# A mixture-of-experts kernel: experts in falling order of count, weights loaded and split inside the tile stage, gathers in four buffers, and a first part that keeps x and h on the chip

## The chip, the cores and the metric

The kernel runs on one core of a Trainium2 chip. A core has TensorE (PE: matrix products; the loading of a stationary operand has rows of its own, PEld), VectorE (DVE), ScalarE (ACT), GpSimd (POOL), and SyncE (SP), which here only issues transfers. 16 DMA engines move the data. Each engine runs its own program in order; they wait for one another on semaphores. The metric is the device time in microseconds.

## What is computed

x has 8 batches of 512 tokens of 256 numbers. Cut from the reference, with B = 8, D = 256, E = 8 experts, FF = 1024 and two experts for each token:

```
h = (x - mu) * rsqrt(var + 1e-05) * ln_g + ln_b            # over the 256 numbers of a token
h_norm = (h - h.mean(1)) * rsqrt(h.var(1) + 1e-08)         # over the 512 tokens of a batch
se = subj_emb[subject_ids]
hyp = relu(se @ hyp_w1 + hyp_b1) @ hyp_w2 + hyp_b2
sty = relu(hyp @ sty_w1 + sty_b1) @ sty_w2 + sty_b2
gamma, beta = split(sty, 2);  gamma = softplus(gamma) + 1e-08
h = h_norm * gamma + beta
probs = softmax(h @ router_w);  gates, idx = top_k(probs, 2);  gates = gates / gates.sum(-1)
hid  = relu(h @ exp_w1[e] + exp_b1[e])
eout = hid @ exp_w2[e] + exp_b2[e]
out  = x + sum over the two experts e of gate * eout
```

## The kernel before, in words

The 8192 pairs of a token and an expert are sorted by expert, each expert's list is filled up to whole tiles of 128, and TILES = 71 tiles are worked through. The program has two stages.

*First part.* For each of the 8 batches of x: statistics of each token (token_stats, VectorE), normalising (normalise, ScalarE), transposing on TensorE (transposes), gain and offset on the way out of PSUM (affine, ScalarE), statistics over the tokens (time_stats, VectorE), modulation with gamma and beta (modulate, GpSimd), logits and transposing back (logits, back, TensorE), copying the rows (rows, ScalarE) and storing them with SyncE into h_rows in memory. x and h have two buffers each on the chip; GpSimd loads x and writes it to out_rows, to which the tiles are added later. Beside this SyncE loads all weights (16 units of 1 MB, one for each of w1 and w2 of an expert) into four stages; ScalarE writes the fp16 high half of a unit (w_hi, 2048 columns) and VectorE the low half (w_lo). Then select picks the two experts of each token, the counts come from a product with ones, and VectorE works out where each expert's list begins. The gates (comb) are stored beside the rows in h_rows.

*Tile stage.* Tile t needs its 128 token numbers (slot_steps and the tokens functions on VectorE, slot_table on TensorE), a gather of the rows by an indirect transfer of GpSimd (gather), two transposes (tile_transpose), halves in fp16 (tile_hi on ScalarE, tile_lo on VectorE), the hidden products (48 of 128 columns) and relu, halves again (split_hi, split_lo), the second products (24 of 256 columns), bias_y on VectorE, the gate (gate_y, ScalarE), and an indirect transfer of GpSimd that adds the 128 rows to out_rows (scatter). Each product of fp32 numbers is three products of fp16 halves.

The order on each engine is written out by hand. In step t TensorE does products(0) (hidden of tile t, first half; second products of tile t-2), tile_transpose(t+1), slot_table(t+3) and products(1). ScalarE does relu of the first half, tile_hi(t+1), gate_y(t-2) and relu of the second half. GpSimd's loop is, before:

```
for t in range(4, TILES + 2):
    scatter(t - 2, (t - 2) % 2)
    if t + 3 < TILES:
        gather(t + 3, (t + 3) % 2)
```

The gathered rows have two buffers, and gather(t+3) waits until the gates of tile t+1 are read (s_gate). scatter(t) waits for yout of its tile (s_yo, by gate_y) and for the landing of the scatter before (s_sc). Ahead of each indirect transfer stands a tiny tensor_tensor that writes held_gp and carries its waits (carry). The line numbers of the profile: 390 gather, 401 scatter, 298 carry, 397 the copy of the scatter's index, 657 tile_transpose, 647 slot_table, 691 and 698 the products, 524 relu, 531 tile_hi, 538 gate_y, 852 w_lo, 474 w_hi, 567 transposes, 577 back, 586 logits, 468 rows, 455 affine.

Of the kernel before, what the change touches and what calls it, by code (L numbers as in the profile page):

```python
# [12 lines left out]
P = 128  # L24
# [18 lines left out]
NSTAGE = 4  # L43
VEC_ROWS = 75
V_LNG, V_LNB, V_HB1, V_HB2, V_SB1, V_SB2 = 64, 66, 68, 69, 70, 71


C_ID, C_SLOT, C_NEGT, C_SLOTCOL, C_Q, C_DJ, C_DESC, C_TOK2, C_T128 = 0, 128, 256, 328, 400, 401, 405, 413, 415
C_END = C_T128 + 72


def moe_kernel(nc, x, ids, ln_g, ln_b, subj_emb, hyp_w1, hyp_b1, hyp_w2, hyp_b2, sty_w1, sty_b1,
               sty_w2, sty_b2, router_w, exp_w1, exp_b1, exp_w2, exp_b2, consts, consts16, out):
# [9 lines left out]
    def w_v(u):  # L63
        return (w2_v if u % 2 else w1_v)[u // 2]

    with ExitStack() as ctx:
# [7 lines left out]

        whi = sb("whi", [P, UNITS * UNIT], F16)
        wlo = sb("wlo", [P, UNITS * UNIT], F16)
        stage = sb("stage", [P, NSTAGE, UNIT])
        cst = sb("cst", [P, C_END])
        c16 = sb("c16", [P, 2 * P], F16)


        xs = sb("xs", [P, 2, JB * D])
        xn = sb("xn", [P, 2, JB * D])
        hT = sb("hT", [P, 2, KD * T])
        hrow = sb("hrow", [P, 2, JB * D])
        hid32 = hT
        hidhi = stage[:, 1, 0:FF].bitcast(F16).rearrange("p (a f) -> p a f", a=2)
        hidlo = stage[:, 2, 0:FF].bitcast(F16).rearrange("p (a f) -> p a f", a=2)
        b2row = hrow[:, :, :].rearrange("p a n -> p (a n)")
        hg = xs[:, 0, 0:2 * HROW].rearrange("p (a d) -> p a d", a=2)  # L90
        ysum = xn[:, 0, 2 * D:4 * D].rearrange("p (a d) -> p a d", a=2)
        yout = xs[:, 1, 0:2 * D].rearrange("p (a d) -> p a d", a=2)
        hThi = xn[:, 0, 0:D].bitcast(F16).rearrange("p (a d) -> p a d", a=2)
        hTlo = xn[:, 0, D:2 * D].bitcast(F16).rearrange("p (a d) -> p a d", a=2)
        step16 = xn[:, 1, 0:2 * P].bitcast(F16).rearrange("p (a h s) -> p a h s", a=2, h=NH)
        junk = xn[:, 1, 2 * P:3 * P]


        hw1 = hrow[0:SE, 1, 0:SH]
        hw2 = hrow[:, 1, SH:2 * SH]  # L100
        sw1 = hrow[:, 1, 2 * SH:2 * SH + SH // 2]
        sw2 = hrow[0:SH // 2, 1, 320:320 + 2 * D]

        d1, d2, ex, oh1 = (xs[:, 0, i * NBLK:(i + 1) * NBLK] for i in range(4))
        tm = xn[:, 1, 3 * P:5 * P]
        sums = xn[:, 1, 5 * P:7 * P]
        csum, dstart = xn[:, 0, 2 * D:3 * D], xn[:, 0, 3 * D:4 * D]
        ones = xn[:, 0, 0:NBLK]
        ge = xs[:, 1, 0:72 * E]


        vrows = sb("vrows", [P, P])
        vcol = sb("vcol", [P, VEC_ROWS])
        rw = sb("rw", [P, KD * E])
        idcol = sb("idcol", [B, 1], I32)
        se = sb("se", [B, SE])
        sT = sb("sT", [P, 4, B])
        gam = sb("gam", [P, KD * B])
        bet = sb("bet", [P, KD * B])
        sp = sb("sp", [P, 6, KD * B])  # L120
        bns = sb("bns", [P, JB, 6])
        mv = sb("mv", [P, 2, JB, 2])
        lnv = sb("lnv", [P, 2, 4, JB])
        tns = sb("tns", [P, KD, 6])
        tmv = sb("tmv", [P, 2, KD, 2])
        tnv = sb("tnv", [P, 2, 6, KD])
        lg = sb("lg", [P, NJ * E])
        selh = sb("selh", [P, NBLK + 1], F16)
        dsel = sb("dsel", [P, NBLK], F16)
        m8 = sb("m8", [P, 8, NJ])  # L130
        start = sb("start", [P, NBLK + 1])
        ne = sb("ne", [P, 6, E])
        nei = sb("nei", [P, 2, E], I32)
        stcol = sb("stcol", [P, 2 * NH])
# [998 lines left out]
```

## Time and profile before

| | |
|---|---|
| median of 3 runs | 545.5 us (543.27 to 732.71) |
| the profiled execution | 544.19 us |
| its span in the trace | 542.5 us |
| TensorE busy | 465.7 us (86%), 5671 instructions |
| VectorE busy | 399.0 us (74%) |
| ScalarE busy | 290.7 us (54%) |
| GpSimd busy | 280.5 us (52%) |
| moved by the DMA engines | 51.36 MB, mean 95 GB/s |

The profile shows one execution. The span goes from its first to its last instruction; the execution's time holds some 1.7 us more. Shares of busy time are means over both stages, so they don't say what bounds either of them; the rows below are taken from single stretches. A busy share of an engine counts neither the issue of plain transfers nor waiting.

### The profile page before, as it was taken

How to read it: one execution, taken by the hardware profiler on the slowest of the kernel's cores; microseconds unless marked ns; L12 is line 12 of the kernel's file. 1: busy time of each engine (PE TensorE's matmuls, PEld its weight loads, DVE VectorE, ACT ScalarE, POOL GpSimd, SP SyncE). 2: the span in 40 equal slices, each digit the busy share in tenths (PEclk: the TensorE clock that was granted, in tenths of full speed). 3: DMA queues.
4: the chain of work that ended last, by engine and by line, in shares of the span. 5: the costliest groups of instructions: out<-in, count | busy, mean ns of one | idle time of the engine just before them, and what ended most of it. 6: DMA issues, size and time to landing. Idle time of an engine off the chain costs nothing.

```text
span 542.5 us, 16211 instructions
## 1 busy us (share of the span) xinstructions
PE 465.7 (86%) x5671; PEld 437.9 (81%) x5671; DVE 399.0 (74%) x1488; ACT 290.7 (54%) x819; POOL 280.5 (52%) x426
## 2 busy tenths in 40 slices
PE   1357666707999999999999999999999999999990
PEld 1356656606999999999999999999999999999990
DVE  3688998897677787777777777777777777877650
ACT  2879877703555455554555545555555554555540
POOL 5032223545465566565665556565556556665542
PEclk9999999999999999999999999999999999999997
DMA  8989996241232322323223232232322323223221
GB/s 270 342 310 323 343 357 213 45 130 29 36 50 50 52 48 48 49 52 51 47 47 51 52 51 47 47 51 51 51 46 48 51 49 53 45 49 51 50 32 19
DMA packets 36417, 51.36 MB, mean 95 GB/s; under 512 B 7804, under 2 KB 29718, under 8 KB 36214
## 3 DMA queue, kind: packets, MB, share of 16 engines
q0 software_dynamic: 16128, 27.59, 25.9%
q1 hardware_dynamic: 20214, 22.78, 12.9%
q8 instruction: 47, 0.77, 0.6%
q14 instruction: 28, 0.23, 0.1%
HBM read 32.24 MB, written 18.11 MB: 93 GB/s over the span
## 4 chain that ended last, share of the span: by engine, by line
PE 76%; DVE 9%; issue 5%; DMA 4%; ACT 2%; POOL 2%; DVEq 0%; POOLq 0%; ACTq 0%
PE bank L691 34%; PE bank L698 33%; PE bank L657 3%; DMA out_rows<-xs 2%; PE bank L647 1%; PE bank L586 1%; DMA xs<-h_rows,idxg 1%; PE bank L567 1%; ACT whi L474 1%; DVE wlo L852 1%; POOL out_rows L401 1%; DMA xs<-in_x 1%; POOL hT L319 1%; DVE xn L950 1%; PE bank L577 1%
## 5 line engine op out<-in xcount | busy, mean ns | idle before, releaser
L698 PE MATMUL bank<-whi,stage 128*128 x1136 | 276.9, 273 | 0.0
L524 ACT ACTIVATE hT<-bank,vcol 128x128 f32<-128x128 f32 x568 | 162.4, 368 | 194.1 <-PE bank L691 194.0
L691 PE MATMUL bank<-xn,whi 128*128 128x128 f16 x2272 | 220.3, 220 | 2.2 <-DVE xn L1004 1.1
L691 PEld LDWEIGHTS bank<-xn,whi 128*128 x2272 | 171.6, 98 | 15.7 <-issue 4.8
L691 PE MATMUL bank<-xn,wlo 128*128 128x128 f16 x1136 | 156.7, 220 | 0.0
L698 PE MATMUL bank<-wlo,stage 128*128 x568 | 154.8, 273 | 0.0
L401 POOL DMA_INDIRECT out_rows<-xs,idxs x71 | 119.4, 1681 | 24.3 <-issue 24.3
L1010 DVE CAST stage<-hT 128x512 f16<-128x512 f32 x142 | 62.0, 437 | 75.6 <-ACT hT L524 61.0
L698 PEld LDWEIGHTS bank<-whi,stage 128*128 128x128 f16 x1136 | 111.1, 98 | 6.6
L298 POOL TENSOR_TENSOR held_gp<-zero 1x1 f32<-1x1 f32 x150 | 36.2, 241 | 133.5 <-DVE tok L996 100.7
L1015 DVE TENSOR_TENSOR stage<-hT,stage 128x512 f16<-128x512 f32 x142 | 96.9, 682 | 0.1
L390 POOL DMA_INDIRECT xs<-h_rows,idxg x71 | 71.0, 1000 | 35.0 <-issue 33.3
L691 PEld LDWEIGHTS bank<-xn,wlo 128*128 x1136 | 87.7, 98 | 0.0
L698 PEld LDWEIGHTS bank<-wlo,stage 128*128 128x128 f16 x568 | 55.6, 98 | 0.1
L1020 DVE SCALAR_TENSOR_TENSOR xn<-bank,hrow 128x256 f32<-128x256 f32 x71 | 30.2, 425 | 20.9 <-PE bank L698 20.9
L968 DVE TENSOR_SCALAR xn<-cst,stcol 128x128 f16<-128x128 f32 x142 | 42.3, 340 | 0.0
L577 PE MATMUL bank<-cst,hT 128*128 128x128 f32 x64 | 15.7, 426 | 29.5 <-POOL hT L319 28.2
L538 ACT ACTIVATE xs<-xn,gates 128x256 f32<-128x256 f32 x71 | 37.8, 532 | 3.1 <-DVE xn L1020 3.1
L577 PEld LDWEIGHTS bank<-cst,hT 128*128 128x128 f32 x64 | 12.7, 226 | 32.3 <-POOL hT L319 22.0
L531 ACT ACTIVATE xn<-bank 128x256 f16<-128x256 f32 x71 | 28.4, 400 | 14.8 <-PE bank L657 14.8
L852 DVE SCALAR_TENSOR_TENSOR wlo<-stage,whi 128x2048 f32 (+1 forms) x14 | 32.0, 2290 | 1.1 <-ACT whi L474 0.4
L657 PE MATMUL bank<-cst,xs 128*128 128x128 f32 x142 | 27.7, 277 | 3.8 <-DMA xs<-h_rows,idxg 3.8
(145 smaller groups left out, 500.3 us busy)
## 6 DMA issues: line engine op xcount, KB each, us to landing
stage<-in_L_cond_exp_w SPq DMA_DIRECT2D x16, 1024.0 KB, 8.6
xs<-in_x POOLq DMA_DIRECT2D x8, 512.0 KB, 6.6
out_rows<-xs POOLq DMA_DIRECT2D x8, 512.0 KB, 7.8
h_rows<-hrow SPq DMA_DIRECT2D x8, 512.0 KB, 10.6
xs<-h_rows,idxg POOLq DMA_INDIRECT x71
out_rows<-xs,idxs POOLq DMA_INDIRECT x71
hrow<-in_L_cond_exp_b SPq DMA_DIRECT2D x1, 1024.0 KB, 4.7
cst<-in_consts SPq DMA_DIRECT2D x1, 243.5 KB
```

Of the source, the lines that this page charges most:

```text
L298: gp.tensor_tensor(held_gp[:, kind:kind + 1], zero[0:1, 0:1], zero[0:1, 0:1], ALU.add).then_inc(s_held[kind], 1)
L390: gp.indirect_dma_start(out=hg[:, par, :], out_offset=None, in_=h_dram, in_offset=bass.IndirectOffsetOnAxis(ap=idxg[par][:, 0:1], axis=0)) ...
L401: gp.indirect_dma_start(out=out, out_offset=bass.IndirectOffsetOnAxis(ap=idxs[par][:, 0:1], axis=0), in_=yout[:, par, :], in_offset=None, ...
L524: ins = nc.scalar.activation(hid32[:, par, c * P:(c + 1) * P], bk_hid[half][:, (c - 4 * half) * P:(c - 4 * half + 1) * P], ACT.Relu, bias= ...
L538: nc.scalar.activation(yout[:, par, :], ysum[:, par, :], ACT.Copy, scale=gates[:, bass.ds(t, 1)]).then_inc(s_yo, 1)
L657: ins = nc.tensor.transpose(bk_g[:, k * P:(k + 1) * P], hg[:, par, k * P:(k + 1) * P], ident)
L691: hid_ins = nc.tensor.matmul(o, lhs[w, k], h[:, par, k * P:(k + 1) * P], start=(n == 0), stop=(n == 3 * KD - 1))
L698: y_ins = nc.tensor.matmul(bk_y[par_y][:, 0:D], h[:, par_y, c * P:(c + 1) * P], rhs[w], start=(n == 0), stop=(n == 3 * FC - 1))
L852: V.scalar_tensor_tensor(out=wlo[:, bass.ds(at, UNIT)], in0=stage[:, slot, :], scalar=WSCALE, in1=whi[:, bass.ds(at, UNIT)], op0=ALU.mult, ...
L968: ins = V.tensor_scalar(step16[:, par, h, :], slotrow, stcol[:, h:h + 1], cst[:, bass.ds(t + C_NEGT, 1)], ALU.subtract, ALU.is_ge)
L1010: V.tensor_copy(hidhi[:, par, a:b], hid32[:, par, a:b]).then_inc(s_dv, 1)
L1015: V.tensor_tensor(hidlo[:, par, a:b], hid32[:, par, a:b], hidhi[:, par, a:b], ALU.subtract).then_inc(s_split, 1)
```

## The change

What it does, part by part:

- *Order of the experts.* After the counts, VectorE sorts the experts by falling count (a key of count and number, max), publishes their numbers in nei (s_ord), and copies the eight parts of selh into that order (selp). SyncE, ScalarE and VectorE read numbers from it into registers. Tiles then come in the order of ranks, and weights lie by rank in whi and wlo.
- *Weights.* None is loaded in the first part. After s_ord SyncE loads eight quarters of the first two units, then stores comb, and loads the other 14 units of 1 MB behind waits for w_lo (three stages). ScalarE and VectorE split the first eight quarters ahead of the tile stage, and in each step t of the tile stage quarter t + 8 (512 columns): w_hi between gate_y and the second relu, w_lo at the end of VectorE's step. GpSimd no longer splits any.
- *First part.* x (8 batches) and h stay on the chip, in the place where weights will lie. Parameters come in one transfer, laid out on the host. Statistics and modulation go by pairs of batches. GpSimd normalises x in place; the statistics over the tokens are read from PSUM; gain, offset and modulation become one pass on ScalarE (modulate). out_rows is filled from x by transfers from memory to memory. Subjects are picked by a product with a one-hot matrix. Probabilities are not divided by their full sum before the two are chosen, since that factor cancels.
- *Gathers.* The gathered rows get four buffers, hg; gather(t) waits for the gates of tile t-4. Four gathers are issued before the loop, and in the loop scatter(t-2) is followed by gather(t+2). The scatter takes its index from tok without a copy.

The diff, cut to the loops of the tile stage, the loading and the splitting:

```diff
+            sp_.wait_ge(s_ord, 1)
+            order = expert_numbers(sp_, nei[0:1, 2, :])
...
+            for i, (u, q) in enumerate(FIRST):
+                src = w_src(u, q)
+                sp_.dma_start(stage[:, u, q * CHUNK:(q + 1) * CHUNK].rearrange("p (a n) -> p a n", a=src.shape[1]),
+                              src).then_inc(s_first[i], 16)
             for part, batches in enumerate((range(0, B - 2), range(B - 2, B))):
...
                 sp_.wait_ge(s_comb, part + 1)
                 for b in batches:
...
+                    sp_.dma_start(comb_v[b], comb[:, b * JB * E:(b + 1) * JB * E].rearrange("p (j e) -> p j e", e=E)).then_inc(s_combst, 16)
+            for u in range(2, UNITS):
+                if u >= NSTAGE:
+                    sp_.wait_ge(s_wlo, NQ * (u - NSTAGE + 1))
+                src = w_src(u)
+                sp_.dma_start(stage[:, u % NSTAGE, :].rearrange("p (a n) -> p a n", a=src.shape[1]), src).then_inc(s_w[u % NSTAGE], 16)
...
+            def normalise(b):
+                gp.wait_ge(s_nrm, b // 2 + 1)
...
-            def gather(t, par):
...
+            def gather(t):
                 gp.wait_ge(s_tok, t + 1)
-                if not (isinstance(t, int) and t < 2):
-
-                    gp.wait_ge(s_gate, t - 1)
+                if t >= 4:
+                    gp.wait_ge(s_gate, t - 3)
                 carry(t, 0)
-                gp.indirect_dma_start(out=hg[:, par, :], out_offset=None, in_=h_dram,
-                                      in_offset=bass.IndirectOffsetOnAxis(ap=idxg[par][:, 0:1], axis=0)).then_inc(s_gh[par], 16)
...
+                gp.indirect_dma_start(out=hg[:, t % 4, :], out_offset=None, in_=h_dram,
+                                      in_offset=bass.IndirectOffsetOnAxis(ap=tok[:, t:t + 1], axis=0)).then_inc(s_gh[t % 4], 16)
...
-                gp.tensor_copy(idxs[par][:, :], tok[:, bass.ds(t, 1)]).then_inc(s_idx, 1)
-                gp.wait_ge(s_idx, t + 1)
                 gp.wait_ge(s_yo, t + 1)
                 carry(t, 1)
...
-            for t in range(5):
-                if t == 2:
-
-                    last_w_lo(1)
-                gather(t, t % 2)
-            for t in range(2, 4):
-                scatter(t - 2, t % 2)
-                gather(t + 3, 1 - t % 2)
-            for t in range(4, TILES + 2):
-                scatter(t - 2, (t - 2) % 2)
-                if t + 3 < TILES:
-                    gather(t + 3, (t + 3) % 2)
+            for t in range(4):
+                gather(t)
+            gp.wait_ge(s_init, 16 * B)
+            for t in range(2, TILES + 2):
+                scatter(t - 2)
+                if t + 2 < TILES:
+                    gather(t + 2)
             gp.wait_ge(s_sc, 16 * TILES)
...
+            for b in range(0, B, 2):
+                time_deviation(b // 2)
+                modulate(b)
+                modulate(b + 1)
...
+                rows(b)
+                rows(b + 1)
...
+                relu(t, t % 2, 0, es[2 + t % 4])
+                if t + 1 < TILES:
+                    tile_hi(t + 1, 1 - t % 2)
+                if t >= 2:
+                    gate_y(t - 2, t % 2)
+                if t + len(FIRST) < UNITS * NQ:
+                    w_hi(t + len(FIRST))
+                relu(t, t % 2, 1, es[2 + t % 4])
...
+                V.scalar_tensor_tensor(out=wlo[:, at], in0=stage[:, u % NSTAGE, q * CHUNK:(q + 1) * CHUNK], scalar=WSCALE, in1=whi[:, at],
+                                       op0=ALU.mult, op1=ALU.subtract).then_inc(s_wlo, 1)
...
+                if t + len(FIRST) < UNITS * NQ:
+                    w_lo(t + len(FIRST))
```

GpSimd's program, before, where the gathers that are issued ahead end and the loop begins. held_gp is the carrier of the waits, DMA xs<-h_rows a gather, DMA out_rows<-xs a scatter. The rows are gather(4), scatter(0), gather(5) and scatter(1):

```order
L298 TENSOR_TENSOR held_gp<-zero 1x1 [waits gather_waits_carried,gates_ready,slot_tokens_ready]
L390 DMA xs<-h_rows,idxg0 128x264
L397 COPY idxs0<-tok 128x1
L298 TENSOR_TENSOR held_gp<-zero 1x1 [waits y_gated,scatter_index_ready]
L401 DMA out_rows<-xs,idxs0 4232x256
L298 TENSOR_TENSOR held_gp<-zero 1x1 [waits gather_waits_carried,gates_ready,slot_tokens_ready]
L390 DMA xs<-h_rows,idxg1 128x264
L397 COPY idxs1<-tok 128x1 [waits y_scattered]
L298 TENSOR_TENSOR held_gp<-zero 1x1 [waits scatter_waits_carried,y_gated,scatter_index_ready]
L401 DMA out_rows<-xs,idxs1 4232x256
```

The same place in the changed kernel, with DMA hg<-h_rows a gather: gather(3), scatter(0), gather(4), scatter(1) and gather(5):

```order
L300 TENSOR_TENSOR held_gp<-zero 1x1 [waits gather_waits_carried,slot_tokens_ready]
L307 DMA hg<-h_rows,tok 128x264
L300 TENSOR_TENSOR held_gp<-zero 1x1 [waits y_gated,out_initialised]
L316 DMA out_rows<-yout,tok 4232x256
L300 TENSOR_TENSOR held_gp<-zero 1x1 [waits gather_waits_carried,gates_ready,slot_tokens_ready]
L307 DMA hg<-h_rows,tok 128x264
L300 TENSOR_TENSOR held_gp<-zero 1x1 [waits scatter_waits_carried,y_gated,y_scattered]
L316 DMA out_rows<-yout,tok 4232x256
L300 TENSOR_TENSOR held_gp<-zero 1x1 [waits gather_waits_carried,gates_ready,slot_tokens_ready]
L307 DMA hg<-h_rows,tok 128x264
```

The copies to idxs are gone, and what follows scatter(0) is gather(4) instead of gather(5).

ScalarE's program in one step of the tile stage, before. The first row is tile_hi, the second gate_y, the others relu of the second half; an ISA row is a piece of register work:

```order
L531 ACTIVATE xn<-bank4 128x256 [waits tile_transposed]
L538 ACTIVATE xs<-xn,gates 128x256 [waits y_scattered,y_biased]
L524 ISA [waits hidden_products]
L524 ACTIVATE hT<-bank1,vcol 128x128
L524 ISA
L524 ACTIVATE hT<-bank1,vcol 128x128
L524 ISA
L524 ACTIVATE hT<-bank1,vcol 128x128
L524 ISA
L524 ACTIVATE hT<-bank1,vcol 128x128
```

ScalarE's program in a step of the changed kernel, again from tile_hi on, then into the first relu of the next step:

```order
L424 ACTIVATE hThi<-bank4 128x256 [waits tile_transposed]
L430 ACTIVATE yout<-ysum,gates 128x256 [waits y_scattered,y_biased]
L412 ACTIVATE whi<-stage 128x512 [waits weights_staged0]
L418 ACTIVATE hid32<-bank1,par 128x128 [waits hidden_products]
L418 ACTIVATE hid32<-bank1,par 128x128 x3
L418 ACTIVATE hid32<-bank0,par 128x128 [waits hidden_products]
```

Behind gate_y stands the high half of a quarter of a weight unit; the order of tile_hi and gate_y is what it was.

## Rows read from the trace of the kernel before

**Rows 1.** Busy time of each engine by stretches: two of 31 and 197 us.

```profile
core 0: us, PE busy (x) PEld busy (x) DVE busy (x) ACT busy (x) POOL busy (x), PEclk, DMA share, GB/s
29.00:60.00 31.00, 20.94 (x96) 19.75 (x96) 28.08 (x78) 25.38 (x38) 7.69 (x14) 1.00 0.94 327
...
133.00:330.00 197.00, 196.96 (x2652) 186.47 (x2650) 146.18 (x590) 102.44 (x348) 116.28 (x172) 1.00 0.29 48
```

**Rows 2.** Timeline of PE: the transposes of steps 2, 31 and 69 (start, us).

```profile
138.37 0.38 PE L657 MATMUL bank<-cst,xs 128*128 128x128 f32 x2
...
302.29 0.38 PE L657 MATMUL bank<-cst,xs 128*128 128x128 f32 x2
...
517.15 0.38 PE L657 MATMUL bank<-cst,xs 128*128 128x128 f32 x2
```

**Rows 3.** Timeline of ACT, step 31: tile_hi and gate_y.

```profile
303.27 0.40 ACT L531 ACTIVATE xn<-bank 128x256 f16<-128x256 f32 x1
303.53 0.53 ACT L538 ACTIVATE xs<-xn,gates 128x256 f32<-128x256 f32 x1
```

**Rows 4.** Timeline of POOL: a slow carrier, and gather and scatter of one step.

```profile
157.44 0.72 POOL L298 TENSOR_TENSOR held_gp<-zero 1x1 f32<-1x1 f32 x1
158.32 1.61 POOL L401 DMA_INDIRECT out_rows<-xs,idxs  x1 [0.16 <-issue]
...
302.34 0.18 POOL L298 TENSOR_TENSOR held_gp<-zero 1x1 f32<-1x1 f32 x1 [1.35 <-DVE tok L996]
303.02 0.99 POOL L390 DMA_INDIRECT xs<-h_rows,idxg  x1 [0.49 <-issue]
304.00 0.20 POOL L397 COPY idxs<-tok 128x1 int32<-128x1 int32 x1
304.29 0.18 POOL L298 TENSOR_TENSOR held_gp<-zero 1x1 f32<-1x1 f32 x1
304.89 1.73 POOL L401 DMA_INDIRECT out_rows<-xs,idxs  x1 [0.42 <-issue]
```

**Rows 5.** The chain that ended last, 119 to 133 us: two gathers, issue to landing.

```profile
119.26 3.06 DMA xs<-h_rows,idxg
...
122.37 0.70 PE bank L657 x2
...
129.90 2.73 DMA xs<-h_rows,idxg
```

**Rows 6.** All scatters of line 401: ns min/median/max, first and last start.

```profile
L401 POOL DMA_INDIRECT out_rows<-xs,idxs x71: 1567/1718/1975, 141.0 to 534.3; - x71
```

**Rows 7.** Groups of instructions: w_lo of a unit, and split_lo (busy us, mean ns).

```profile
L1015 DVE TENSOR_TENSOR stage<-hT,stage 128x512 f16<-128x512 f32 x142 | 96.9, 682 | 0.1
...
L852 DVE SCALAR_TENSOR_TENSOR wlo<-stage,whi 128x2048 f32 x12 | 27.5, 2291 | 0.9 <-ACT whi L474 0.2
```

**Rows 8.** Timeline of the first part: back, logits, rows, affine of one batch.

```profile
30.65 1.97 PE L577 MATMUL bank<-cst,hT 128*128 128x128 f32 x8 [10.48 <-POOL hT L319]
...
32.41 3.42 PE L586 MATMUL bank<-rw,hT 128*128 128x8 f32 x16
...
35.09 1.05 ACT L468 ACTIVATE hrow<-bank 128x512 f32<-128x512 f32 x2
...
37.67 1.45 ACT L455 ACTIVATE hT<-bank,vcol 128x512 f32<-128x512 f32 x2 [1.44 <-PE bank L567]
```

**Rows 9.** Timeline between the stages: stores of comb, a VectorE subtraction, the first products.

```profile
104.10 4.25 SPq L272 DMA_DIRECT2D h_rows<-xs  x6
...
109.72 4.16 DVE L950 TENSOR_TENSOR xn<-start 128x256 f32<-128x256 f32 x1
...
124.42 0.60 PE L691 MATMUL bank<-xn,whi 128*128 128x128 f16 x4 [1.15 <-DVE xn L1004]
```

**Rows 10.** Timeline of PE: four hidden products early in the tile stage.

```profile
125.03 0.63 PE L691 MATMUL bank<-xn,whi 128*128 128x128 f16 x4
...
128.73 0.39 PE L691 MATMUL bank<-xn,whi 128*128 128x128 f16 x4
...
130.84 0.39 PE L691 MATMUL bank<-xn,whi 128*128 128x128 f16 x4 [0.94 <-issue]
```

More of the change, by code:

```diff
@@ L337, in _ @@
+            for b in range(B):
+                normalise(b)
             held = [0]
@@ L625, in _ @@
-            for b in range(B - 2, B):
-                back(b, b % 2)
-            pe.wait_ge(s_cst16, 16)
-            pe.wait_ge(s_sel, 2)
-            nc.tensor.matmul(bk_cnt[:, 0:NBLK], ones16, selh[:, 1:NBLK + 1], start=True, stop=True).then_inc(s_cnt, 1)
+            pe.wait_ge(s_cst16, 16)
+            pe.wait_ge(s_par, 16)
+            pe.wait_ge(s_hot, 1)
+            MM(bk_small[0:SE, 0:B], subj, onehot[:, 1, :], start=True, stop=True).then_inc(s_sty_pe, 1)
+            pe.wait_ge(s_sty_a, 1)
@@ new lines, in _ @@
+            ins.then_inc(s_sty_pe, 1)
+            pe.wait_ge(s_cst, 16)
+            transposes(0)
+            transposes(1)
+            for b in range(0, B - 2, 2):
+                transposes(b + 2)
+                transposes(b + 3)
+                for i in (b, b + 1):
+                    logits(i)
+                    back(i)
+            for b in (B - 2, B - 1):
+                logits(b)
+            for b in (B - 2, B - 1):
+                back(b)
+            pe.wait_ge(s_sel, 2)
@@ new lines, in _ @@
+            link(ins)
+            for k in range(E):
+                ins = V.tensor_copy(selp[:, 1 + k * NJ:1 + (k + 1) * NJ], selh[:, bass.ds(order[k] * NJ, NJ)])
+            ins.then_inc(s_perm, 1)
+            ve.wait_ge(s_perm, 1)
+            V.tensor_tensor(dsel[:, :], selp[:, 1:NBLK + 1], selp[:, 0:NBLK], ALU.subtract).then_inc(s_ds, 1)
+            ve.wait_ge(s_ccol, 1)
+            V.tensor_tensor(ca16[:, :], bk_col[:, 0:NH], adj[:, 0, :], ALU.add).then_inc(s_ca, 1)
+            ve.wait_ge(s_col, 1)
@@ L1044, in _ @@
                 if t == 0:
-                    tile_experts()
-                if t == 1:
-                    tile_lo(0, 0)
-            ve.wait_ge(s_b2, 16)
-            def step(t, par, at, e, e_y):
-                def tile(u):
-                    return not isinstance(u, int) or 0 <= u < TILES
-                other, tokens = 1 - par, tile(t + 3)
-                gate(t, par, e)
-                if tile(t - 2):
-                    bias_y(t - 2, par, e_y)
-                if tile(t + 4):
+                    w_lo(0)
+                    w_lo(1)
+            w_lo(2)
+            w_lo(3)
+            tile_lo(0, 0)
+            for i in range(4, 8):
+                w_lo(i)
+            tile_experts()
+            at += 1
+            tile_experts_done(at)
+            ve.wait_ge(s_b2, 16)
+            es = [order[0]] * 6
+            for t in range(TILES):
+                if t >= 8 and t % 4 == 0:
+                    if t == 8:
+                        ve.wait_ge(s_et, 1)
+                    es = expert_numbers(ve, etile[0:1, t:t + 6])
+                par, other, tokens = t % 2, 1 - t % 2, t + 3 < TILES
+                gate(t, es[2 + t % 4])
+                if t >= 2:
+                    bias_y(t - 2, par, es[t % 4])
+                if t + 4 < TILES:
                     slot_steps(t + 4, par)
```

1087 lines of the change are left out of this document (498 added, 589 removed).

## The prediction

> **What bounds the kernel now.** I read the stretches first, to see which stage is bound by what. While h is built (29 to 60 us) TensorE is busy 20.94 of 31 us and the DMA engines 0.94 of the time; in the tile stage TensorE is busy 196.96 of 197 us, VectorE 146.18, ScalarE 102.44 and GpSimd 116.28 [rows 1]. So up to about 100 us the transfers set the pace, and from 133 us on TensorE does. Its pace in that stage is read from the pair of transposes that stands in the middle of each step. Call the time at which step t transposes tile t+1 M(t). M(2) is 138.37 and M(69) is 517.15, so 67 steps take 378.8 us, 5.65 each [rows 2]. The kernel before is therefore M(2) = 138.4, plus 67 times 5.65, plus 25.35 from M(69) to the end of the span: 542.5. Then I read GpSimd's row of events in one step, because it starts both indirect transfers of a tile and the change rewrites its loop.
>
> **The one step that decides: the gather has moved by one tile.** In both kernels ScalarE's step t does, in order, relu, tile_hi(t+1), which needs M(t), and gate_y(t-2); GpSimd's scatter(t-2) waits for that gate_y. In step t the trace shows M(t) at 302.29 [rows 2], tile_hi(t+1) at 303.27, gate_y(t-2) at 303.53 [rows 3], and scatter(t-2) starting at 304.89, which is M(t) + 2.6 [rows 4]. Before, what follows it on GpSimd is gather(t+3), whose rows are first needed at M(t+2), 11.3 us after M(t). Now it is gather(t+2), needed at M(t+1). Four row buffers instead of two don't help, since the queue on GpSimd is a fixed order. So a closed chain appears that goes round once per tile: M(t), tile_hi(t+1), gate_y(t-2), scatter(t-2), gather(t+2), M(t+1). Its length, from rows:
> - rows landed to TensorE's start, 0.05: a gather that starts at 119.26 lands 3.06 later, and the transposes start at 122.37 [rows 5];
> - the two transposes, 0.38 [rows 2];
> - tile_hi to the start of gate_y, 0.26, and gate_y, 0.53 [rows 3];
> - held_gp before the scatter to the scatter's start, 0.60 (304.29 to 304.89), and 0.88 where held_gp itself ran long (157.44 to 158.32) [rows 4];
> - the scatter's own time on GpSimd, 1.72 by its median [rows 6];
> - held_gp before the gather to the gather's start, 0.68 (302.34 to 303.02) [rows 4];
> - the gather's start to its landing, 3.06 and 2.73 [rows 5]; I take 2.9.
>
> That is 0.05 + 0.38 + 0.79 + 0.60 + 1.72 + 0.68 + 2.9 = 7.12; three more handovers between engines at the 0.05 of the first line give 7.25 us, against 5.65. The copy to idxs (0.20 [rows 4]) is already left out. The shortest chain (2.73, no handovers) is 6.95, the longest (0.88, 3.06, handovers) 7.7, and a gather that shares the DMA engines with a weight transfer may be later still: 7.9. Every one of them is above 5.65, so TensorE stops in front of the transposes of each tile for about 1.6 us. The first four gathers are issued ahead, and gather(4) is the first one behind a scatter, which is needed at M(3); so the chain holds from M(2) to M(69): 67 x 7.25 = 486 us instead of 379, **+107 us**.
>
> The Trainium skill, "DMA: Bandwidth & Descriptors", Anatomy of one DMA — SWDGE (gpsimd) path, gives 2.0 us plus bytes / 436e3 for such a transfer, some 2.3 us for 128 rows of 1,056 bytes. By it the chain would be 6.65 and the result about 608 us; this case's gathers took 2.73 and 3.06, so the measurement decides.
>
> **The other parts of the change.**
> - Splitting weights in the tile stage. Each of the first 56 steps gets one w_hi of 512 columns on ScalarE and one w_lo on VectorE. A whole w_lo took 2.29 us for 2048 columns, a tensor_tensor of 512 columns 0.68 [rows 7]: I take 0.68. VectorE's load per tile is 146.18 / 197 x 5.65 = 4.19 [rows 1]; less the index that is written twice today (0.15, an estimate), plus 0.68, it is 4.7, under 5.65 and far under 7.25: nothing. Without that cover it would cost at most 56 x 0.68 = 38 us. ScalarE has still more room. The split lies behind the last index of a step, so the instruction that queues behind it is the next tile's gate and bias_y.
> - Loading weights there: 14 transfers of 1 MB where the queues are slack. They wait on w_lo and nothing but weights waits behind them on SyncE. Chunk 8r + 3 is split in step 8(r - 1) + 3 and needed in step 8r: five steps early.
> - The products: the same 48 and 24 matmuls per tile, no gain. Registers of expert numbers are read at the same steps.
> - The new first part. It drops 16 MB of weights, so the transfers no longer bound it; a serial chain per pair of batches does. ScalarE takes rows(2i+1) before the square root of the next pair: 1.05, about 1.3 for the root and the five small VectorE steps behind it (an estimate), modulate 1.45, two batches of transposes at 1.97, and logits and back for two batches, 2 x (3.42 + 1.97) [rows 8]: 18.5 us a pair. With the first logits at about 38 us (statistics of two pairs and the style network lie ahead; 35 to 42), the third pair's back ends at 86, the last rows are transposed back at about 101, near 105.4 before. From there the first index took until 118; the instruction of 4.16 us is gone [rows 9], while the sorting of the experts, the register reads and the eight copies of selh come in, some 4 us. SyncE now issues eight weight pieces and only then the eight stores of comb, at 4.25 / 6 = 0.7 each [rows 9], before the first gather may start: it starts at 114 to 118. From a first gather (119.26 [rows 5]) to the first product (124.42 [rows 9]) it is 5.2, and 13.95 more to M(2). So M(2) lies at 133 to 137; I take 135, a gain of 3, and 127 to 145 as its bounds.
> - The end: three scatters, each behind the landing of the one before; two index copies less, 0.4.
>
> **Sum.** 135 + 486 + 25.35 - 0.4 = 646 us of span; the profiled execution took 544.19 for its 542.5, so + 1.7 = **648 us**. The median of the runs, 545.5, stands 1.3 above that execution. A measurement of this kernel can tell about 2% from no change, 11 us.
>
> **Rivals.**
> - The gather comes in time after all. It decides at 1.6 us: if a gather landed 1.3 us after its start, or if a scatter held GpSimd for 0.1 us, the chain would be 5.65 and TensorE would be the bound again: 135 + 379 + 25 + 1.7 = 541, and some 545 if every fourth step, where experts are read, delays tile_lo. Against it stand both landings and a scatter row that never falls under 1.57 [rows 6]. This is also the case in which the change is not slower. 8%.
> - TensorE's clock falls because of the new stops. Four products take 0.63 us at 125.03 and 0.39 at 128.73; after a stop of 0.94 they still take 0.39 [rows 10]. Where TensorE was idle a third of the time, a batch's eight transposes took 1.97, 0.22 apart [rows 8], while two take 0.38 in the tile stage [rows 2]. So 1.2 GHz comes back somewhere between a stop of 0.94 us in steady work and the first part's pattern, and 1.6 us per 7.25 lies between. The granted clock of both stretches reads 1.00 [rows 1], so it is the durations that show it. At 1.2 GHz a tile is 11.3; with half of the steps there, 135 + 67 x 9.3 + 27 = 785 us. The Trainium skill, "TensorE: Matmul & The Clock Gate", A second HAM failure mode: psum-queue depth-cycling, reports this for frequent short stops; the gap at 130.84 speaks against it. 7%.
> - The first part gains much more, say 25 us, because its pairs overlap better. Even then it is 623; it can't turn the sign.
>
> **Chances.** The chain as the bound has 85%. Its range takes 6.95 with M(2) at 127 and 7.9 with 145: 127 + 466 + 27 = 620 and 145 + 529 + 27 = 701. Both named rivals lie outside, 15%, and I leave 4% for sizes past the ends. Faster by over 2% has 3%, within 2% has 5%, slower 92%.
>
> **What would show it.** Right: a wait of TensorE's transposes for the gathered rows on 66 or more tiles, 1.3 to 2.2 us each; TensorE's share of the tile stage near 78%; step spacing of 7.25; scatter and gather next to each other on GpSimd, which then waits for gate_y. Wrong: spacing of 5.65 with transposes that never wait, or four products at 0.6 us in the middle of the tile stage.

## The result, and the profile after

The changed kernel takes 647.2 us (median of 4 runs, 644.1 to 653.2) against 544.4 us: ratio 1.191, 95% interval 1.179 to 1.203. The forecast was 648. The profiled execution took 644.08 us, its span is 642.2. Below, medians are over all executions of a kernel while ratios leave out those more than 1.5% above its fastest; their first part came later, so the tile stage is compared by its own spacing.

First the stretches, as in [rows 1], from the windows view of the changed kernel:

```profile
29.00:60.00 31.00, 19.01 (x128) 18.54 (x128) 21.41 (x93) 10.61 (x19) 9.55 (x19) 0.84 0.36 122
133.00:330.00 197.00, 163.23 (x2075) 147.15 (x2073) 127.70 (x462) 97.13 (x301) 88.88 (x109) 0.98 0.35 76
```

The DMA share of the first stretch has fallen from 0.94 to 0.36: the weights are gone from there. In the tile stage no engine is full any more. TensorE, busy 196.96 of 197 us before, is busy 163.23, or 83%. When every engine has room and the stage is longer, something goes round. The waits say where it closes (who waited for whom, us in total, times, longest):

```profile
POOL held_gp L300 <- issue: 242.9, 68, 4.6
...
PEld bank L543 <- DMA hg<-h_rows,tok: 110.9, 62, 10.8
PE bank L543 <- DMA hg<-h_rows,tok: 93.6, 62, 10.5
```

Line 543 is the pair of transposes of a tile. It waits for gathered rows on 62 tiles, 10.5 of the 93.6 us once, for tile 0. GpSimd in turn waits 68 times in front of a scatter, 3.6 us on average. The view names no releaser for it ("issue"), but held_gp, which carries the wait for gate_y, starts 0.13 or 0.14 us after the end of gate_y in each of 67 steps. The transposes themselves, from the timeline of TensorE; they answer to [rows 2]:

```profile
130.91 0.38 PE L543 MATMUL bank<-cst,hg 128*128 128x128 f32 x2
138.47 0.44 PE L543 MATMUL bank<-cst,hg 128*128 128x128 f32 x2 [1.76 <-DMA hg<-h_rows,tok]
...
303.90 0.44 PE L543 MATMUL bank<-cst,hg 128*128 128x128 f32 x2 [1.06 <-DMA hg<-h_rows,tok]
310.81 0.44 PE L543 MATMUL bank<-cst,hg 128*128 128x128 f32 x2 [1.05 <-DMA hg<-h_rows,tok]
...
617.26 0.44 PE L543 MATMUL bank<-cst,hg 128*128 128x128 f32 x2 [1.07 <-DMA hg<-h_rows,tok]
```

M(2) is 130.91 and M(69) 617.26, so a step takes 486.35 / 67 = 7.26 us, and 25.0 us lie behind M(69). The stop begins at M(3), the first tile whose gather is queued behind a scatter.

One round of the chain, between the two rows in the middle: first two of ScalarE's rows, then GpSimd's.

```profile
304.38 0.38 ACT L424 ACTIVATE hThi<-bank 128x256 f16<-128x256 f32 x1 [0.59 <-PE bank L543]
304.66 0.50 ACT L430 ACTIVATE yout<-ysum,gates 128x256 f32<-128x256 f32 x1
```

```profile
305.29 0.61 POOL L300 TENSOR_TENSOR held_gp<-zero 1x1 f32<-1x1 f32 x1 [3.24 <-issue]
306.06 1.60 POOL L316 DMA_INDIRECT out_rows<-yout,tok  x1 [0.16 <-issue]
307.11 0.61 POOL L300 TENSOR_TENSOR held_gp<-zero 1x1 f32<-1x1 f32 x1
307.96 1.00 POOL L307 DMA_INDIRECT hg<-h_rows,tok  x1 [0.24 <-issue]
```

Read downwards: transposes at 303.90, tile_hi 304.38, gate_y 304.66, held_gp 305.29, scatter 306.06, gather 307.96, and the next transposes, which need the rows of that gather, at 310.81. The pieces are 0.48, 0.28, 0.63, 0.77, 1.90 and 2.85: 6.91 us. Between scatter and gather GpSimd rests for 0.24.

7.26 is a mean over unequal steps. Of 67, 37 take 6.80 to 7.05 and 30 take 7.27 to 8.26: there a gather landed late, or TensorE was slow behind a longer stop, or the scatter came later after M(t). The section on the prediction returns to these.

### The profile page after: what moved, and what is told of

Its sections match the earlier page's. It is cut to its first block and busy times, and to the rows that moved or that the text cites. A ratio compares the mean times of both kernels' runs of the same rounds, so it can differ in the third digit from the quotient of the medians.

```text
span 642.2 us, 15826 instructions
## 1 busy us (share of the span) xinstructions
PE 477.2 (74%) x5679; PEld 431.7 (67%) x5679; DVE 386.0 (60%) x1436; ACT 282.6 (44%) x832; POOL 251.2 (39%) x331
## 5 line engine op out<-in xcount | busy, mean ns | idle before, releaser
L418 ACT ACTIVATE hid<-bank,par 128x128 f32<-128x128 f32 x568 | 161.9, 368 | 213.0 <-PE bank L588 213.0
L588 PE MATMUL bank<-hThi,whi 128*128 128x128 f16 x1136 | 191.4, 222 | 5.3 <-DVE hTlo L843 4.4
L588 PE MATMUL bank<-hTlo,whi 128*128 128x128 f16 x1136 | 191.6, 222 | 0.0
L588 PE MATMUL bank<-hThi,wlo 128*128 128x128 f16 x1136 | 159.1, 222 | 0.0
L595 PE MATMUL bank<-whi,hidhi 128*128 (+1 forms) x568 | 157.3, 277 | 0.0
L595 PE MATMUL bank<-wlo,hidhi 128*128 (+1 forms) x568 | 157.3, 277 | 0.0
L595 PE MATMUL bank<-whi,hidlo 128*128 (+1 forms) x568 | 156.9, 276 | 0.0
L588 PEld LDWEIGHTS bank<-hThi,whi 128*128 (+1 forms) x1136 | 112.4, 99 | 14.7 <-DVE hTlo L843 5.0
L316 POOL DMA_INDIRECT out_rows<-yout,tok x71 | 114.2, 1608 | 14.0 <-issue 13.6
L588 PEld LDWEIGHTS bank<-hTlo,whi 128*128 (+1 forms) x1136 | 112.9, 99 | 6.2
L543 PE MATMUL bank<-cst,hg 128*128 128x128 f32 x142 | 31.0, 300 | 93.6 <-DMA hg<-h_rows,tok 93.6
```

The lines of the kernel that those rows point to most:

```text
L316: gp.indirect_dma_start(out=out, out_offset=bass.IndirectOffsetOnAxis(ap=tok[:, t:t + 1], axis=0), in_=yout[:, t % 2, :], in_offset=None, ...
L418: ins = S(hid32[:, par, c * P:(c + 1) * P], bk_hid[half][:, (c - 4 * half) * P:(c - 4 * half + 1) * P], ACT.Relu, bias=vcol[:, bass.ds(e * ...
L543: ins = nc.tensor.transpose(bk_g[:, k * P:(k + 1) * P], hg[:, t % 4, k * P:(k + 1) * P], ident)
L588: hid_ins = MM(o, lhs[w, k], h[:, par, k * P:(k + 1) * P], start=(n == 0), stop=(n == 3 * KD - 1))
L595: y_ins = MM(bk_y[par_y][:, 0:D], h[:, par_y, c * P:(c + 1) * P], rhs[w], start=(n == 0), stop=(n == 3 * FC - 1))
```

## Experiments

**1. The gather in front of the scatter.** If the chain is closed by the order of two calls, turning them round opens it: the gather then waits for neither scatter nor gate_y.

```diff
             for t in range(2, TILES + 2):
-                scatter(t - 2)
                 if t + 2 < TILES:
                     gather(t + 2)
+                scatter(t - 2)
```

> The changed kernel with one thing moved: in GpSimd's loop gather(t+2) stands ahead of scatter(t-2) instead of behind it. Theory A, the closed chain over scatter and gather: it is cut, the transposes never wait for rows, the step spacing is 5.65 us, and with the changed kernel's M(2) = 130.9 and its end, 24.8, the span is 131 + 67 x 5.65 + 25 = 535 us, the time 537. Theory B, the stops come from the weight transfers and the splitting that now lie in the tile stage: spacing stays above 6.9 us and the time above 620 us.

Measured: 554.5 us (546.0 to 558.0, 8 runs), ratio 1.013 (1.008 to 1.017); M(2) is 143.11 and M(69) 531.56, so 5.80 us a step. Two swapped calls give back 98 of 108 us (67 times 7.26 less 5.80, and less 5.65). The rest was not expected, and 554.5 misses theory A's 537: transposes still waited ten times, up to 1.17 us, and M(2) came 12 us late.

**2. The old distance.** Five gathers ahead of the loop, and gather(t+3) behind the scatter, as the kernel before does, in the changed kernel.

```diff
-            for t in range(4):
+            for t in range(5):
                 gather(t)
...
-                if t + 2 < TILES:
-                    gather(t + 2)
+                if t + 3 < TILES:
+                    gather(t + 3)
```

> The changed kernel with the old lead: five gathers ahead and gather(t+3) behind scatter(t-2), with the four buffers and all the rest as changed. Theory A: gather(t+3) now waits for the token numbers of the step, but is needed 11.3 us after M(t); 5.65 us a step and 537 us, as in the run beside it, within 3 us. Theory B: above 620 us.

552.7 us (546.2 to 556.3, 4 runs), 5.79 us a step from M(2) = 136.01. The chain is gone here too, and the same 0.14 us a step over the kernel before is left, so this run misses its 537 as well. The two experiments are less different than they look. In both the gather starts as soon as its token numbers are there, in most steps 5.0 to 5.4 us before the transposes that need it; gather(t+3) doesn't start a step earlier than gather(t+2) does in experiment 1.

**3. The chain alone, in the kernel before.** Nothing of the change but the distance: four gathers ahead and gather(t+2) behind the scatter, with the old first part and no weights in the tile stage.

```diff
-            for t in range(5):
+            for t in range(4):
...
-                if t + 3 < TILES:
-                    gather(t + 3, (t + 3) % 2)
+                if t + 2 < TILES:
+                    gather(t + 2, (t + 2) % 2)
```

> The kernel before with the new lead alone: four gathers ahead and gather(t+2) behind scatter(t-2); weights, first part, two buffers and the index copy stay as before. Theory A: the chain appears here too, 6.9 to 7.3 us a step, so 138 + 67 x (6.9 to 7.3) + 25 + 2 = 627 to 654 us. Theory B: no weights move in this tile stage, so 544 us stay.

653.3 us, ratio 1.201 (1.199 to 1.204): the whole loss, and a little more, from this edit. M(2) is 137.68, M(69) 626.40: 7.29 us a step, a mixture of 34 steps of 6.87 to 7.04 and 33 of 7.1 to 8.1, as in the changed kernel. The loss appears in full without the splitting, the loading and the new first part.

**4. A longer chain.** A fill of 768 columns with its wait, between scatter and gather.

```diff
                 scatter(t - 2)
                 if t + 2 < TILES:
+                    link(gp.memset(par_[:, P_HW1:P_HW1 + 768], 0.0))
                     gather(t + 2)
```

> The changed kernel with a memset of 768 columns and its wait on GpSimd between scatter(t-2) and gather(t+2), some 0.9 to 1.1 us by the 0.34 us that a memset of 264 columns took in the first part. Theory A: it lies in the chain, so every step from M(2) to M(69) grows by its length: 60 to 75 us more than the changed kernel, 705 to 722 us. If GpSimd had room there: under 5 us more.

719.8 us, 8.29 a step: +1.03 for a fill that takes 1.32 and partly runs beside the scatter. From M(t) to the gather's start it is 5.04 us on average in place of 4.12, so 0.92 of the 1.03 lie where the fill was put; the other 0.12 are gathers that took longer to be used.

**5 and 6. Weights in quarters.** In experiment 1 the late gathers stood beside weight transfers. Its rows, from the timelines of GpSimd, SyncE's queue and TensorE:

```profile
271.30 1.00 POOL L307 DMA_INDIRECT hg<-h_rows,tok  x1 [0.16 <-issue]
...
271.29 0.38 SPq L254 DMA_DIRECT2D stage<-in_exp_w  x1
...
277.94 0.44 PE L543 MATMUL bank<-cst,hg 128*128 128x128 f32 x2 [1.17 <-DMA hg<-h_rows,tok]
```

The gather lands 6.6 us after its start where 2.85 is usual. All ten stops belong to gathers beside which a 1 MB transfer started, 0.01 to 0.18 us earlier. So both orders were run with the same megabytes cut into pieces of 256 KB, one a step:

```diff
-            for u in range(2, UNITS):
+            for i in range(len(FIRST), UNITS * NQ):
+                u, q = i // NQ, i % NQ
...
-                sp_.dma_start(stage[:, u % NSTAGE, :]...).then_inc(s_w[u % NSTAGE], 16)
+                sp_.dma_start(stage[:, u % NSTAGE, q * CHUNK:(q + 1) * CHUNK]...).then_inc(s_w[i % (NSTAGE * NQ)], 16)
```

> The changed kernel with the gather of tile t+2 ahead of the scatter of tile t-2 (as in the earlier run with that order), and the weights of the tile stage loaded in quarters of 256 KB, one a step, in place of 1 MB every fourth step. Theory A: what was left of the step over the kernel before (5.80 against 5.65 us) is gathers that land late because a 1 MB transfer sits in the same DMA engines. With quarters the waits of the transposes shrink to under 0.2 us each, spacing 5.65 to 5.70 us, so the tile stage is 7 to 10 us shorter than with whole megabytes, and the time is 540 to 548 us. Theory B: the waits come of the gather's own long landings, whatever is loaded beside it: spacing stays 5.78 to 5.82 us and the time 550 to 556 us.

542.1 us (10 runs), ratio 0.994 (0.990 to 0.999); no transposes of the loop wait for a gather, 5.67 us a step.

> The changed kernel with five gathers ahead of the loop and gather(t+3) behind scatter(t-2), weights in quarters. Theory A as for the run before: waits of the transposes for the gather vanish (a gather starts a whole step earlier than it is needed), spacing 5.65 to 5.70 us, time 538 to 548 us, which would be level with the kernel before. Theory B: spacing stays at 5.79 us, time 550 to 556 us.

538.0 us (534.6 to 540.9, 4 runs), ratio 0.989 (0.981 to 0.998); M(2) = 129.77, M(69) = 509.68, 5.67 a step. Its windows row, and GpSimd's rows for one step:

```profile
133.00:330.00 197.00, 196.30 (x2641) 185.81 (x2639) 162.93 (x590) 120.37 (x384) 128.04 (x139) 1.00 0.45 94
```

```profile
300.51 0.99 POOL L309 DMA_INDIRECT hg<-h_rows,tok  x1
302.07 0.18 POOL L302 TENSOR_TENSOR held_gp<-zero 1x1 f32<-1x1 f32 x1 [0.57 <-issue]
302.77 1.78 POOL L318 DMA_INDIRECT out_rows<-yout,tok  x1 [0.51 <-issue]
305.71 0.56 POOL L302 TENSOR_TENSOR held_gp<-zero 1x1 f32<-1x1 f32 x1 [1.16 <-DVE tok L831]
306.43 1.16 POOL L309 DMA_INDIRECT hg<-h_rows,tok  x1 [0.15 <-issue]
```

TensorE is full again (196.30 of 197) although it now shares the stage with 14 MB of weights and their split. GpSimd waits for tok ahead of a gather, with time to spare, in place of gate_y. Theory A holds for both. The gathers start 4.9 to 5.6 us before their transposes here too, not a whole step more than in experiment 5 as the expectation has it.

**7 and 8. No weight transfers at all.** In the order of experiment 1 and in the changed kernel, the transfers from the fourth unit on are left out; the stages are split again with what they hold, so most products use wrong weights.

```diff
-            for u in range(2, UNITS):
+            for u in range(2, 3):
...
-                    act.wait_ge(s_w[u % NSTAGE], 16 * len(range(2 + (u - 2) % NSTAGE, u + 1, NSTAGE)))
+                    act.wait_ge(s_w[2], 16)
```

> The kernel with the gather ahead of the scatter, and the plain weight transfers from the fourth unit on left out; the stages are split again with what they hold, so the products use wrong weights and the output is not the reference's. Theory A (the 1 MB transfers delay the gathers): no transpose waits over 0.2 us for a gather, spacing 5.65 to 5.68 us, and the time is 8 to 10 us below the same order with the transfers. Theory B (own long landings): spacing 5.75 to 5.82 us, and the time falls by under 3 us.

545.7 us; 5.67 us a step (M(2) = 138.90, M(69) = 518.97) and no wait for a gather: the same as with quarters. The whole megabytes cost 0.13 us a step, 8 us; cut into quarters they cost nothing.

> The changed kernel itself with the same transfers left out (weights wrong, output not the reference's). Theory A (the chain through scatter and gather sets the step, the transfers have no part in it): spacing 7.15 to 7.3 us, time 636 to 648 us. Theory B (a gather slowed by a weight transfer sets the step): spacing falls to 6.2 us or less, time under 580 us.

644.1 us against 647.2; 7.14 us a step, a hair under the range given. Without the transfers it is 0.12 us a step less, 8 us of a loss of 108, and that is the most that can be put down to them: these are two single executions, and they differ also in how often TensorE was slow behind a stop (6 steps against 3). In the changed kernel the megabyte started some 2 us or more behind the gather that it stood beside, in experiment 1 less than 0.2 us ahead of it. Long landings stay without the transfers.

**9. The fill off the chain.** Experiment 4's fill, in the order of experiment 1.

```diff
                 if t + 2 < TILES:
                     gather(t + 2)
+                    link(gp.memset(par_[:, P_HW1:P_HW1 + 768], 0.0))
                 scatter(t - 2)
```

> The order with the gather of tile t+2 ahead of the scatter of tile t-2, and the same fill of 768 columns with its wait put between the two. In the changed kernel that fill lengthened the step by 1.03 us. Theory A (the step was set by a closed loop through scatter and gather, and with the gather in front that loop is open): the fill only delays the scatter, which nobody waits for; spacing 5.78 to 5.85 us, time 546 to 558 us, that of the same order without the fill. Theory B (GpSimd's own work per step sets the spacing): GpSimd holds about 1 us more in every step, spacing 6.2 us or more, time over 580 us.

571.6 us (571.0 and 572.3), 6.02 us a step: neither theory. The step grew by 0.22 us, not by 1.03 and not by nothing. GpSimd has room, it waits for tok 65 times. The groups of VectorE show where the time is, here and, in the second fence, in experiment 1 (busy us, mean ns):

```profile
L801 DVE TENSOR_SCALAR step<-cst,stcol 128x128 f16<-128x128 f32 x124 | 86.6, 1152 | 0.0
...
L849 DVE CAST hidhi<-hid 128x512 f16<-128x512 f32 x125 | 63.0, 504 | 20.2 <-ACT hid L419 19.1
```

```profile
L848 DVE CAST hidhi<-hid 128x512 f16<-128x512 f32 x129 | 57.1, 442 | 73.2 <-ACT hid L418 73.2
L800 DVE TENSOR_SCALAR step<-cst,stcol 128x128 f16<-128x128 f32 x128 | 39.7, 352 | 0.0
```

The same instruction took 1152 ns in place of 352. Within this run the fill is what tells them apart: 122 of the comparisons from 133 to 530 us overlap a fill and take 1215 ns on average, the 10 that don't take 340. The two of a step overlap each other, so the pair holds VectorE for 86.6 / 62 = 1.40 us in place of 39.7 / 64 = 0.62, some 0.8 more a step, and VectorE, busy 156.39 us between 133 and 330 us in experiment 1, was busy 178.13 here. So this fill wasn't time on GpSimd alone, and experiments 11 and 12 replace it. Nor was it the same time: the fill took 0.75 us here and 1.32 in the chain. In experiment 4 no comparison lay beside a fill, and they took 335 ns.

**10. The version of experiment 6 again,** for a tighter ratio.

> The kernel with gather(t+3) behind the scatter and the weights in quarters once more, for a tighter ratio to the kernel before: 0.985 to 0.995, 535 to 541 us. Its spread comes from the first part, whose pace on TensorE differs from run to run: the tile stage is to take 5.67 us a step in every run, and the time is about 24 us behind M(69).

541.0 us (535.1 to 547.2, 10 runs), ratio 0.991 (0.988 to 0.995). M(2) = 135.13, M(69) = 515.02: 5.67 a step.

**11 and 12. Time on GpSimd without traffic.** Six fills of one column, each with its wait, in the two places.

```diff
+                    for i in range(6):
+                        link(gp.memset(par_[:, P_HW1 + i:P_HW1 + i + 1], 0.0))
```

> The changed kernel with six fills of one column, each with its wait, between the scatter of tile t-2 and the gather of tile t+2: time on GpSimd without the traffic of the 768-column fill. The six should take 0.6 to 1.2 us together. Theory A (closed loop through GpSimd): the step grows by about what they take, less the rest between scatter and gather that they cover, 7.7 to 8.4 us a step, 675 to 725 us. Theory B (the 768-column fill counted in the chain only because it slowed VectorE): the step stays within 0.15 us of 7.26, under 660 us.

760.3 and 783.6 us, above the range; the profile is that of the longer run. M(2) is 138.98 and M(69) 756.48, 9.22 us a step. Theory B has fallen, as the 335 ns of experiment 4 already said, and theory A's size was off. The six took 1.4 to 1.7 us together in place of 0.6 to 1.2. The trace splits the 1.96 us by which the step grew: from M(t) to the gather's start it is 5.68 us in place of 4.12, which is 1.55 for the fills in the chain, and from there to the transposes 3.54 in place of 3.13, which is 0.40 for later landings. Most of the latter is nine steps of 11.5 to 12.5 us, with a stop of some 6. In them a 1 MB transfer starts with the gather, for example at 307.04 and 306.54, and the transposes follow at 312.84. Behind the last of these, from 548 us on, the steps are 8.25 to 9.7.

> The same six fills between gather(t+2) and scatter(t-2) in the order with the gather in front. With the 768-column fill in this place the step was 6.02 us in place of 5.80 and VectorE's counts of slots took 1152 ns in place of 352. Theory A (that fill held VectorE up; time on GpSimd alone is free here): VectorE's counts are back at 350 to 450 ns, spacing 5.75 to 5.85 us, time 546 to 560 us. Theory B (a later scatter costs by itself): spacing stays at 6.0 us or more, 565 us or more.

565.1 and 566.1 us, inside theory B's range for the time but not for the spacing. VectorE's counts are back at 342 ns, as theory A has it, but the mean step is 5.90, above what A gave. Theory A's time was also missed because the first part was late: M(2) is 143.81, as in the 558.0 us execution of experiment 1. There are eleven waits of the loop's transposes for gathers, 0.3 to 1.65 us and 10.9 us together, against ten stops and 5.7 us in experiment 1. All of them stand beside a 1 MB transfer, which starts less than 0.2 us ahead of the gather as it does there; why they are longer was not found. From 425 us on, when the weights are all there, no transposes wait and a step takes 5.71 us against 5.66 in experiment 1. So the six fills, 0.9 us here, cost 0.05 us a step by themselves off the chain, and 1.55 for the 1.4 to 1.7 us that they take in it.

## Why the prediction was right

- **The closed chain, M(t) to gather(t+2) to M(t+1).** Right, and shown from three sides: it appears alone in the kernel before (experiment 3), opens when either call is moved (1 and 2), and pays for what is put in it (4 and 11).
- **Its length, 7.25.** The terms as listed add up to 7.12 + 0.15 = 7.27. The mean is 7.26, but for a reason that is partly luck. A plain round takes 6.91. The term that was too long is scatter to gather: 1.72 + 0.68 = 2.40 in the sum, 1.90 measured. The prediction added the scatter's whole duration from [rows 6] to the held_gp behind it; in the rows above, held_gp starts at 307.11, 1.05 after the scatter's start and inside its 1.60, and nothing stands between the two on GpSimd now. The way from M(t) to the scatter was 2.16 against 0.38 + 0.79 + 0.60 = 1.77 and 0.1 of handovers: the fixed waits between engines were too small. The prediction had a sign of this in its own rows, a scatter at M(t) + 2.6, and didn't ask why its terms gave less. The gather's 2.85 to the transposes was near 2.9 and 0.05. The missing 0.35 x 67 = 23 us came back from things that had been given as ends of the range or as a rival, or not at all: 13.9 us from 14 late gathers, 2.5 from six rounds in which TensorE itself was late, 4.5 from gathers that started later after M(t), the rest in small parts.
- **The later starts.** They are a second length of the chain, which the prediction didn't see. Where TensorE stopped in front of M(t), the scatter starts 2.16 us after it in nearly every step; in the seven steps without such a stop it starts at 2.6, as it did in the kernel before. One of them is M(t) = 210.26: ScalarE's relu of the first half runs from 210.23 to 211.37, so gate_y starts at 211.51 and the scatter at 212.87. The stop had given ScalarE the time to finish that relu first. So a stop shortens the round behind it, by 0.45 us.
- **Late gathers.** The step of 7.9 "that shares the DMA engines with a weight transfer" exists in length, but the weights are a third of the excess at most (7.26 to 7.14 in experiment 8). In the changed kernel the transposes came over 3.5 us after the start of their gather in 14 of 67 steps. (Taken from the gather's start to the transposes' start, which is the landing wherever TensorE was waiting.) In each of the 14 one packet of 16 KB of the queue "q8 instruction" started 1.1 to 2.0 us after the gather, and the transposes came 1.26 to 1.41 us after the end of that packet. In the other 53 no such packet started over 0.2 us after the gather, and they took 2.79 to 3.37; in seven of them one had started earlier or with it. One of the 14, a gather that started at 199.07 (the stretch 199.97 to 202.67 of the DMA view):

```profile
q0 software_dynamic: 152, 0.23, 40.9%
q1 hardware_dynamic: 79, 0.08, 23.0%
q8 instruction: 1, 0.02, 2.1%
...
hg<-h_rows,tok POOLq DMA_INDIRECT x1, 3.8
```

  Without weight transfers (experiment 8) it is again 14 with such a packet, 3.44 to 4.16, the transposes again 1.26 to 1.41 us behind its end, and 53 without, 2.76 to 3.28. So a gather in flight when such a packet moves is used some 0.6 to 1.3 us later than the usual 2.87. That is a coincidence without an exception in 134 gathers; no run took the packets away, so the cause is not shown beyond it.
- **TensorE's clock, a rival at 7%.** It was real in small. After the stop of 2.05 us in front of 202.92, products came 0.42 us long in place of 0.27 until about 206.9, and the step had no wait at the gather behind it because TensorE itself was late:

```profile
202.92 0.44 PE L543 MATMUL bank<-cst,hg 128*128 128x128 f32 x2 [2.05 <-DMA hg<-h_rows,tok]
...
203.75 0.42 PE L595 MATMUL bank<-whi,hidhi 128*128 x1
...
207.28 0.27 PE L595 MATMUL bank<-whi,hidhi 128*128 x1
```

  That happened in 6 of 67 steps, after stops of 1.82 to 2.34 us. It is no clean line: after 8 other stops of 1.84 to 2.19 us the products stayed at 0.27. After shorter ones, 1.06 among them, they always did. It never held for half of the steps, so 785 us was far off.
- **M(2), taken as 135.** 130.91 in the profiled execution; see the section on the first part.
- **Splitting in the tile stage costs nothing.** Right: without the chain the step is 5.67 against 5.65 (experiments 5, 6 and 7).
- **Loading weights there costs nothing.** Wrong by up to 8 us in the steps, where the prediction had looked only at who waits on SyncE. It mattered when the megabyte starts. Where it started between 0.2 us ahead of a 128-row gather and 0.7 behind it and TensorE waited, the transposes came 5.3 to 6.9 us after the gather's start (experiments 1, 2, 11 and 12); where it started 1.6 us or more behind it, as in the changed kernel, the gathers without an instruction packet took 2.8 to 3.3.
- **The end, 24.95.** 25.0.
- **What would show it.** Spacing, the neighbours on GpSimd and the wait for gate_y came as written. Waits of 66 or more tiles at 1.3 to 2.2 us were 61 (tile 0 apart), 34 of them at 0.9 to 1.2, because the plain round is shorter than forecast and in six steps TensorE itself was late. Its share was 83% and not 78%, though the mean step was as forecast: it was busy some 6.0 us a step in place of 5.65. The slow products are a part of that; the rest wasn't taken apart.

## The first part, and what it gave

In the runs of the changed kernel and its variants M(2) lies anywhere from 128 to 144. Two kernels with the same first part, up to the loading of the weights, show the larger part of it: the one of experiment 6, then the one of experiment 7, TensorE's timeline for the first two batches.

```profile
36.86 3.65 PE L466 MATMUL bank<-cst,whi 128*128 128x128 f32 x16 [9.58 <-ACT whi L382]
40.30 1.91 PE L474 MATMUL bank<-par,whi 128*128 128x8 f32 x16
42.07 1.07 PE L484 MATMUL bank<-cst,whi 128*128 128x128 f32 x8
```

```profile
35.74 3.65 PE L464 MATMUL bank<-cst,whi 128*128 128x128 f32 x16 [9.25 <-ACT whi L380]
39.18 3.42 PE L472 MATMUL bank<-par,whi 128*128 128x8 f32 x16
42.45 1.95 PE L482 MATMUL bank<-cst,whi 128*128 128x128 f32 x8
```

After the same 16 transposes the logits took 1.91 in one execution and 3.42 in the other, and back 1.07 and 1.95. That is near the 2 to 1 of TensorE's two levels, 2.4 and 1.2 GHz. The prediction had taken 3.42 and 1.97 from [rows 8], where the kernel before runs at the slower pace, and came to 135. M(2) goes with how early the faster pace begins:

| the first of three pairs of batches with logits under 3.42 us | M(2) |
|---|---|
| the first (changed kernel, experiments 4, 5, 6) | 128.0 to 132.9 |
| the second (2, 10) | 135.1 and 136.0 |
| the third (8, 9, 11) | 135.4 to 140.7 |
| none (1, 7, 12) | 138.9 to 143.8 |

What decides the pace wasn't found. Within a row of the table the first gather makes a difference. Tile 0 was transposed 6.1 to 6.5 us after its gather's start with whole megabytes, 3.7 to 4.0 with quarters (5, 6, 10) and 3.4 to 3.6 without transfers (7, 8). So the whole megabytes cost some 2.5 us more there, which the prediction didn't have either.

Against 138.37 before, M(2) is 2 to 10 us earlier in seven of the twelve profiled executions with the new first part, 7.5 in the changed kernel's, and up to 5 us later in the other five. The first part is the only part of the change that can give time: the tile stage, with the chain opened and the weights in quarters, is level at 5.67 a step. That version (experiments 6 and 10) takes 0.989 and 0.991 of the time of the kernel before; by the medians of all executions, 538.0 and 541.0 us against 543.4 and 543.8, it is 0.990 and 0.995. That is a gain of about 1% at most, under the 2% that the prediction names as what can be told from no change. Experiment 5, at 0.994 with the same tile stage, can't be told from it.

## What to carry to other kernels

A queue that is a fixed order on one engine closes loops that no buffer count opens. When a load is moved nearer to its use, write down the round (use, what its step releases, what stands ahead of the next load in the same queue, the load's landing), sum it, and compare it with the busiest engine's step: 7 against 5.65 us said all of this case's loss. Then cut large background transfers into pieces, or start them well behind a small transfer that something waits for: a megabyte that started together with a gather delayed it by 2.5 us and more, one that started 2 us behind it hardly at all.

## What the runs showed of the hardware

- 256 KB pieces that started with 128-row gathers cost nothing measurable (5.67 us a step with them and without). 1 MB pieces that started with them brought the rows 5.3 to 6.9 us after the gather's start; the same pieces 1.6 us or more behind the gather left most at 2.8 to 2.9.
- A gather during which a 16 KB instruction packet started, over 1 us behind the gather's own start, took 3.44 us or more, and its rows were used 1.26 to 1.41 us after the packet's end; every other one took 3.37 or less (134 gathers in two runs).
- A carrier on GpSimd started 1.05 us after the start of a scatter whose own row is 1.60 us long: the row's length is not what the scatter adds to a chain.
- Beside a fill of 768 columns on GpSimd VectorE's 128-column comparison took 1215 ns on average, in the same run without one beside it 340; fills of one column left it at 342. The fill itself took 0.75 us there and 1.32 behind the start of a scatter.
- The granted clock in the profile's rows did not tell TensorE's pace. In the stretch from 36 to 50 us it read 0.62 where the first logits took 1.91 us (experiment 6), and 1.00 where they took 3.42 (experiment 7); in experiment 10, where they took 3.42 as well, it read 0.50:

```profile
36.00:50.00 14.00, 10.55 (x64) 10.18 (x64) 7.66 (x38) 5.03 (x11) 4.31 (x8) 0.62 0.33 114
```

```profile
36.00:50.00 14.00, 13.41 (x64) 13.01 (x63) 5.38 (x28) 2.88 (x7) 4.33 (x8) 1.00 0.25 76
```
